# Causal attention on one Trainium2 core: value products of two rounds issued together, projections parted anew between the rounds

## The chip, the cores and the metric

The kernel runs on one NeuronCore of one Trainium2 chip. TensorE multiplies and transposes, VectorE and ScalarE read its results out of PSUM, GpSimd works on SBUF only, and SyncE starts transfers. The metric is the device time of one execution in microseconds (us); less is better. All of the five engines run programs of their own, which meet only through semaphores.

## The reference, cut to what matters

Two decoder layers on x of 2 x 1024 x 256 in float32: a recurrence, a cross attention and a ternary feed forward, then a causal self attention, a second cross attention and a quantized gated feed forward, each followed by a layer norm. The change touches only the causal self attention of the second layer, 16 heads of 64 over 1024 positions, for 2 batches:

```
q = jnp.einsum('qdh,bcd->bhcq', Q, x) * sq
k = jnp.einsum('qdh,bcd->bhcq', K, x) * sq
v = jnp.einsum('vdh,bcd->bhcv', V, x) * sv
att = jnp.einsum('bhcq,bhCq->bhcC', q, k) / d_query
att = jnp.where(causal, att, -jnp.inf)
p = jax.nn.softmax(att, axis=-1)
y = jnp.einsum('bhcC,bhCv->bhcv', p, v)
z = jnp.einsum('dvh,bhcv->bcd', W, y) * (math.sqrt(d_embed / d_value) / num_heads)
x = _layernorm(x + z)
```

## The kernel before

A pair of heads in one batch is a unit u; there are 2 x 8 = 16 units. A unit has eight query tiles qt of 128 rows, and tile qt looks at qt + 1 key blocks of 128. `causal_rounds` (line 1645) packs tiles so that each round has eight key blocks for each of the two heads: (4,2), (5,1), (6,0) and (7) of unit u, then (3) of u together with (3) of u + 1, then (4,2), (5,1), (6,0), (7) of u + 1. These are nine rounds for two units and 72 rounds in all, numbered n = 0 to 71.

One order of steps, written by `causal_order` (line 1535), is walked by every engine; an engine executes the steps for which it has a handler, in that order, and skips the rest. The steps of round n are:

- `cs(n)`: TensorE computes the scores of both heads, 64 x 128 weights, into banks 0 to 3 (line 1742); VectorE adds the causal mask and takes the row maxima, head 0 first (lines 1875 and 1877); ScalarE takes the first exponential (line 1812). A score matmul waits until the exponential of round n - 1 has read the same bank (line 1740).
- `cp(n - 2)`: TensorE multiplies the turned probabilities by the values, two heads side by side in 64 columns each, into bank 6 (line 1767).
- `cn(n, 0)`, `cn(n, 1)`: VectorE takes the reciprocals (line 1888); GpSimd scales head 0 (line 1919), VectorE head 1 (line 1894).
- `ct(n - 1)`: TensorE transposes the 16 blocks of round n - 1 in four groups of four, head 1 first (line 1754). ScalarE copies groups 0 and 1 to SBUF (line 1825), VectorE group 2 (line 1882).
- `ce(n)`: ScalarE takes the other exponentials, head 0 and then head 1, at most two each.
- `cy(n - 2)`: ScalarE copies the result of the value products out of bank 6 (lines 1832 and 1838). `ctl(n - 1)`: ScalarE copies group 3 of the transposes.
- `beside[n]`: the projections of later units: `cq`, `ck`, `cv`, each for half of the 1024 positions (lines 1704, 1715 and 1728; copied out by ScalarE, VectorE and VectorE, lines 1794, 1854 and 1859). There are 12 for nine rounds. Transposes of weights (`flip`) stand there in rounds 10 to 13, and the output products of batch 0 (`zout`, line 1782) with their norm from round 37 on.

Transposes, projections, flips and output products share the three banks 4, 5 and 7 in turn (lines 1579 to 1603): an entry waits for the copy of the third entry before it. So group 3 of `ct` takes the bank of group 0, the first projection behind it that of group 1, and a second one that of group 2.

```
        for key, name, value in ends:
            if key in k.room:
                continue
            n = len(causal) % 3
            causal.append(key)
            k.room[key] = ((4, 5, 7)[n], *free[n])
            free[n] = (name, value)
```

Of the kernel before, what the change touches and what calls it, by code (L numbers as in the profile page):

```python
# [16 lines left out]
P = 128  # L17
# [8 lines left out]
HP = H // 2  # L26
# [36 lines left out]
class Order:  # L63
# [13 lines left out]
    def at(self, *step):  # L77
        return self.number[step]
# [39 lines left out]
def lane_of(L, T):  # L118
    return {0: T % LANES, 1: T // BT, 2: T // BT, 3: 2 + T // BT, 4: T % WIDE, 5: OUTPUTS.index(T) % LANES if T < BT else T % LANES, 6: 0, 7: T % LANES}[L]

# [1414 lines left out]
def causal_order(k):  # L1535
    o = k.order
    n0 = len(k.flips)
    for n, p in enumerate(range(0, HP, 2)):
        k.flip_of("wz", [k.wzp[c][:, q * P:(q + 1) * P] for q in (p, p + 1) for c in range(DC)],
                  k.WzT[:, p:p + 2, :].rearrange("p q d -> p (q d)"), 4 + n % 2, ("vector", "scalar")[n % 2])  # L1540
    wz = [[("wzp",)]] + [[("flip", n)] for n in range(n0, len(k.flips))]
    o.add(("causal_load", 2), ("causal_setup",))

    rounds = causal_rounds()
    beside = [[] for _ in rounds]
    for u in range(0, 2 * HP, 2):
        n = ROUNDS * u // 2
        for gap, x in ((0, ("cq", u + 1, 0)), (0, ("ck", u + 1, 0)), (1, ("cq", u + 1, 1)), (2, ("ck", u + 1, 1)), (3, ("cv", u + 1, 0)), (4, ("cv", u + 1, 1)),
                       (4, ("cq", u + 2, 0)), (5, ("ck", u + 2, 0)), (6, ("cq", u + 2, 1)), (7, ("ck", u + 2, 1)), (8, ("cv", u + 2, 0)), (8, ("cv", u + 2, 1))):
            if x[1] < 2 * HP:  # L1550
                beside[n + gap].append(x)
    for i, steps in enumerate(wz):
        beside[ROUNDS + i] += steps
    ahead = HP // 2 * ROUNDS + 1
    for i, T in enumerate(OUTPUTS):
        chain, n = list(norm_chain(5, T)), ahead + i // 2
        beside[n] += [("zout", T)] + chain[:3]
        beside[n + 1].append(chain[3])
        beside[n + 2] += chain[4:]
    o.add(("cq", 0, 1), ("ck", 0, 1), ("cv", 0, 1))  # L1560
    for n in range(len(rounds)):
        o.add(("cs", n))
        if n >= 2:
            o.add(("cp", n - 2))
        o.add(("cn", n, 0))
        if n >= 1:
            o.add(("ct", n - 1))
        o.add(("ce", n))
        if n >= 2:
            o.add(("cy", n - 2))  # L1570
        if n >= 1:
            o.add(("ctl", n - 1))
        o.add(("cn", n, 1), *beside[n])
    n = len(rounds) - 1
    o.add(("ct", n), ("ctl", n), ("cp", n - 1), ("cy", n - 1), ("cp", n), ("cy", n))
    o.meet()

    k.turned = {by: sum(k.flips[x[1]][4] == by for x in o.steps if x[0] == "flip") for by in ("scalar", "vector")}
    k.piece, causal, free, made = {}, [], [("c.q", 0)] * 3, [0, 0]
    for step in o.steps:  # L1580
        ends = []
        if step[0] in ("cq", "ck", "cv"):
            ends = [(step, "c." + step[0][1], o.at(*step))]
        elif step[0] == "zout" and step[1] < BT:
            ends = [(step, "ln.r", o.at("r", 5, step[1]))]
        elif step[0] == "flip" and k.flips[step[1]][0] == "wz":
            by = k.flips[step[1]][4]
            ends = [(step, "flip." + by, sum(k.flips[x[1]][4] == by for x in o.steps if x[0] == "flip" and x[1] <= step[1]))]
        elif step[0] == "turn" and step[1] == 5 and step[2] < BT:
            ends = [(step, "ln.put", o.at("put", *step[1:]))]  # L1590
        elif step[0] == "ct":
            for i in range(len(causal_groups(step[1]))):
                by = int(i != 2)
                made[by] += 1
                k.piece[step + (i,)] = (("vector", "scalar")[by], made[by], sum(made))
                ends.append((step + (i,), ("c.pT.vector", "c.pT.scalar")[by], made[by]))
# [7 lines that stand above are left out]
# [35 lines left out]


ROUNDS = 9
OUTPUTS = (4, 2, 5, 1, 6, 0, 7, 3)


# [36 lines left out]
def causal_column(n, t):  # L1681

    tiles = causal_rounds()[n]
    return 1 - t if len(tiles) == 2 and tiles[0][0] == tiles[1][0] else t
# [8 lines left out]
def causal_tensor(e, w, k):  # L1693
    sem, at, PS, rounds = k.sem, k.order.at, k.PS, Rounds()
# [62 lines left out]
    def cp(n):  # L1757
        for i in range(len(causal_groups(n))):
            by, m, _ = k.piece["ct", n, i]
            w.wait_ge("c.pT." + by, m)  # L1760
        w.wait_ge("c.y", n)
        for t, u, qt, start in rounds.places(n):
            w.wait_ge("c.v", at("cv", u, qt // 4))
            c = causal_column(n, t) * P
            for j in range(qt + 1):
                for h in range(2):
                    y = e.matmul(PS[h * 64:(h + 1) * 64, 6, c:c + P], k.V[u % 2][:, j, h * 64:(h + 1) * 64], k.pT[n % 2][:, (1 - h) * BT + start + j, :],  # L1767
                                 start=j == 0, stop=j == qt, skip_group_check=True)
        y.then_inc(sem("c.pv"), 1)

    def zout(T):
        t, bank = T % BT, T % 2
        w.wait_ge("c.y", ROUNDS * HP // 2 * (T // BT + 1))
        for by in ("scalar", "vector"):
# [13 lines left out]
def causal_scalar(e, w, k):  # L1788
    sem, at, PS, rounds = k.sem, k.order.at, k.PS, Rounds()
# [3 lines left out]
        w.wait_ge("t2.conv", len(k.conv_pe))  # L1793
        e.mul(k.qT[u % 2][:, blk * 512:(blk + 1) * 512], PS[:, k.room["cq", u, blk][0], :], -1.0 / 256).then_inc(sem("c.q"), 1)

    def cs(n):
        if n >= 2:
            w.wait_ge("c.turn", k.piece["ct", n - 2, len(causal_groups(n - 2)) - 1][2])
        exps(n, 0, (0,))
# [27 lines left out]
    def cy(n):  # L1827
        tiles = rounds.tiles[n]
        (u, qt), (v, low) = tiles[0], tiles[-1]
        w.wait_ge("c.pv", n + 1)  # L1830
        if len(tiles) == 1:
            e.copy(k.YT[:, u % HP, qt * P:(qt + 1) * P], PS[:, 6, 0:P]).then_inc(sem("c.y"), 1)
            return
        if u == v:
            dst = k.YT[:, u % HP, :].rearrange("p (t q) -> p t q", q=P)[:, low:qt + 1:qt - low, :]
        else:
            dst = k.YT[:, u % HP:v % HP + 1, qt * P:(qt + 1) * P]
        e.copy(dst, PS[:, 6, 0:2 * P].rearrange("p (t q) -> p t q", q=P)).then_inc(sem("c.y"), 1)  # L1838

    return {"cq": cq, "cs": cs, "ce": ce, "ct": ct, "ctl": ctl, "cy": cy}  # L1840


def causal_vector(e, w, k):
# [52 lines left out]
    def r(L, T):  # L1896
        w.wait_ge("c.zout", at("zout", T))
        if T in OUTPUTS[LANES:]:
            w.wait_ge("ln.unit", at("unit", 5, OUTPUTS[OUTPUTS.index(T) - LANES]))
# [799 lines left out]
```

## Time and profile before

| | |
|---|---|
| median of 3 runs | 2013.95 us (2013.32 to 2014.62) |
| profiled execution | 2018.72 us |
| its span from the first to the last instruction | 2016.9 us |
| mean granted TensorE clock | 0.924 |
| busy: TensorE matmul | 1747.6 us (87%) |
| busy: VectorE | 1388.2 us (69%) |
| busy: ScalarE | 1014.5 us (50%) |
| busy: GpSimd | 456.4 us (23%) |
| causal rounds 0 to 71 in the profile | about 765 to 1405 us |

Times are in us from the start of the span. In rows of the timeline a group of like instructions is merged; the first number is its start and the second its length. Matmuls are pipelined, so the distance from one group's start to the start of the next is what the group costs, more than its printed length. PE is TensorE's matmul, PEld its weight load, DVE VectorE, ACT ScalarE, POOL GpSimd. READ_ACCUMULATOR rows are the last part of the instruction before them.

### The profile page before, as it was taken

The numbers are of one execution on the slowest core, as the hardware profiler recorded it, in microseconds if no ns is written. First come the engines' busy times: TensorE is split into PE (matmuls) and PEld (weight loads), VectorE is DVE, ScalarE is ACT, GpSimd is POOL, SyncE is SP. The second block draws the span as 40 slices with busy tenths as digits, with TensorE's granted clock in tenths as the row PEclk, the third lists the DMA queues.
The fourth block names the chain that finished last, engine by engine and source line by source line (L and its number), as shares of the span: only waits on it lengthen the run. The fifth ranks groups of instructions, "written<-read, shape, count | busy, mean of one in ns | idle before, by whom it ended". The sixth has DMA issues, their size and how long they took to land.

```text
span 2016.9 us, 34705 instructions
## 1 busy us (share of the span) xinstructions
PE 1747.6 (87%) x12889; PEld 1267.5 (63%) x12889; DVE 1388.2 (69%) x4850; ACT 1014.5 (50%) x2639; POOL 456.4 (23%) x493
## 2 busy tenths in 40 slices
PE   3678988888878889999999999999879999989808
PEld 1356766666653455667667766667559899974307
DVE  6888888887236886777776577776446767653685
ACT  5645556555338534555553455554135545433752
POOL 4000000000000323333343333333113232320003
PEclk8778888888979989999999999999989999999959
DMA  5000000000000101000000000001323342400001
GB/s 160 1 1 1 1 1 1 1 1 1 1 1 22 21 21 69 1 1 1 1 1 1 1 1 1 2 1 38 101 63 78 82 95 65 95 1 0 0 0 42
DMA packets 86078, 49.56 MB, mean 25 GB/s; under 512 B 40223, under 2 KB 83669, under 8 KB 85717
## 3 DMA queue, kind: packets, MB, share of 16 engines
q1 hardware_dynamic: 80195, 47.18, 9.1%
q8 instruction: 102, 1.67, 0.3%
q10 hardware_dynamic: 5714, 0.16, 0.2%
q14 instruction: 67, 0.55, 0.1%
HBM read 45.24 MB, written 2.10 MB: 23 GB/s over the span
## 4 chain that ended last, share of the span: by engine, by line
PE 58%; DVE 27%; ACT 9%; issue 3%; POOL 2%; DMA 1%; ACTq 0%; DVEq 0%; POOLq 0%
PE PS L2063 6%; PE PS L1742 6%; DVE nx L764 6%; DVE sq L773 6%; PE PS L1754 5%; PE PS L1767 4%; PE PS L2481 3%; ACT px L1812 3%; PE PS L1728 3%; PE PS L1704 3%; PE PS L2126 3%; PE PS L1782 2%; PE PS L1715 2%; PE PS L2082 2%; PE PS L2091 2%
## 5 line engine op out<-in xcount | busy, mean ns | idle before, releaser
L1812 ACT ACTIVATE px<-PS,cnm 128x896 f32<-128x896 f32 (+7 forms) x256 | 189.4, 756 | 285.5 <-DVE cnm L1877 285.5
L1919 POOL TENSOR_SCALAR px<-px,crl 128x640 f32<-128x640 f32 (+7 forms) x128 | 232.5, 1826 | 371.2 <-DVE crl L1888 371.2
L773 DVE TENSOR_SCALAR sq<-nx 128x4 f32<-128x4 f32 x1024 | 174.3, 170 | 31.3
L764 DVE TENSOR_TENSOR_SCAN nx<-sq 128x6 f32<-128x6 f32 x1024 | 173.0, 169 | 32.0 <-POOL sq L903 0.9
L1875 DVE TENSOR_REDUCE cm<-PS 128x1 f32<-128x512 f32 (+3 forms) x224 | 153.7, 686 | 44.6 <-PE PS L1742 44.6
L1754 PE MATMUL PS<-ident,px 128*128 128x128 f32 x1152 | 156.1, 281 | 9.3 <-ACT pT L1825 6.2
L198 POOL TENSOR_SCALAR rstd<-mv 128x1 f32<-128x1 f32 x80 | 34.0, 425 | 533.7 <-DVE mv L176 533.7
L2153 ACT ACTIVATE YT<-YT,xnm 128x154 f32<-128x154 f32 x256 | 104.8, 413 | 92.7 <-DVE xnm L2195 92.7
L1742 PE MATMUL PS<-kT,qT 64*128 64x512 f32 (+3 forms) x768 | 147.9, 503 | 0.4
L1754 PEld LDWEIGHTS PS<-ident,px 128*128 128x128 f32 x1152 | 124.1, 141 | 36.6 <-ACT pT L1825 23.9
L1767 PEld LDWEIGHTS PS<-pT,V 128*64 128x64 f32 x2304 | 124.8, 137 | 34.4 <-issue 32.5
L1767 PE MATMUL PS<-pT,V 128*64 128x128 f32 x2304 | 142.1, 276 | 0.6 <-ACT YT L1838 0.6
L1825 ACT COPY pT<-PS 128x512 f32<-128x512 f32 x216 | 122.4, 603 | 7.4 <-PE PS L1754 7.4
L1742 PEld LDWEIGHTS PS<-kT,qT 64*128 64x128 f32 x768 | 67.1, 186 | 80.0 <-issue 44.4
L1894 DVE TENSOR_SCALAR px<-px,crl 128x640 f32<-128x640 f32 (+7 forms) x128 | 108.6, 884 | 2.5
L205 POOL TENSOR_SCALAR rstd<-lst 128x1 f32<-128x1 f32 x48 | 9.3, 194 | 424.4 <-ACT ljunk L264 422.7
L1149 DVE TENSOR_REDUCE nnm<-PS 128x1 f32<-128x154 f32 x256 | 72.7, 308 | 43.2 <-PE PS L1014 42.8
L2242 POOL TENSOR_TENSOR YT<-YT,xrl 128x1024 f32<-128x1024 f32 x32 | 60.8, 1899 | 176.4 <-DVE YT L2204 176.4
L1888 DVE RECIPROCAL crl<-cl 128x2 f32<-128x2 f32 (+1 forms) x144 | 23.8, 165 | 97.5 <-ACT px L1812 97.5
L1877 DVE CUSTOM_DVE_ANT_0 PS<-PS,cmask,cm 128x128 f32<-128x128 f32 x224 | 80.5, 359 | 7.9
L818 PE MATMUL PS<-XT,W1T 128*128 128x256 f32 x256 | 64.9, 399 | 4.2 <-ACT XT L288 2.4
L2208 DVE COPY YT<-PS 128x512 f32<-128x512 f32 x80 | 51.9, 681 | 21.5 <-PE PS L2091 21.5
(339 smaller groups left out, 3882.8 us busy)
## 6 DMA issues: line engine op xcount, KB each, us to landing
xbs<-in_fside_Bx16xSxS SPq DMA_DIRECT2D x8, 1232.0 KB, 6.8
fsrc<-in_fside_Bx16xSxS SPq DMA_DIRECT2D x8, 1232.0 KB, 6.7
xmk<-in_mask_Bx16xSxS_bk SPq DMA_DIRECT2D x8, 308.0 KB, 8.6
fsrc<-in_mask_Bx16xSxS_bk SPq DMA_DIRECT2D x8, 308.0 KB, 8.4
X<-in_x SPq DMA_DIRECT2D x4, 512.0 KB, 6.7
w<-in_L_attn_W_ffn SPq DMA_DIRECT2D x2, 1024.0 KB, 12.6
t<-in_L_ffn_w SPq DMA_DIRECT2D x2, 1024.0 KB, 11.9
out<-xs SPq DMA_DIRECT2D x16, 128.0 KB, 1.7
```

The source lines that it names most:

```text
L764: e.tensor_tensor_scan(k.nx[:, t % 2, :], d0, d1, 0.0, ALU.mult, ALU.add).then_inc(sem("rec.scan"), 1)
L773: e.tensor_scalar(place(c % 2 * 2 * W6 + 6 * n + 7), state, 10.0, -10.0, ALU.min, ALU.max).then_inc(sem("rec.clip"), 1)
L1742: y = e.matmul(PS[:, 2 * h + lo // 512, lo % 512:lo % 512 + hi - lo], k.qT[u % 2][rows_, qt * P:(qt + 1) * P], k.kT[u % 2][rows_, lo - c0: ...
L1754: y = e.transpose(PS[:, bank, q * P:(q + 1) * P], k.px[n % 2][:, h, (starts[t] + j) * P:(starts[t] + j + 1) * P], k.ident[:, :])
L1767: y = e.matmul(PS[h * 64:(h + 1) * 64, 6, c:c + P], k.V[u % 2][:, j, h * 64:(h + 1) * 64], k.pT[n % 2][:, (1 - h) * BT + start + j, :], st ...
L1812: e.activation(k.px[n % 2][:, h, c0:c1], row[:, c0:c1], ACT.Exp, scale=-1.0, bias=k.cnm[:, h, slot:slot + 1], accum_out=k.cl[:, h, slot:sl ...
L1825: e.copy(k.pT[n % 2][:, 4 * i:4 * i + len(group), :].rearrange("p b q -> p (b q)"), PS[:, k.room["ct", n, i][0], 0:len(group) * P]).then_i ...
L1875: e.tensor_reduce(most, row[:, start * P:mid], AX.X, ALU.min).then_inc(sem("c.before"), 1)
L1894: e.tensor_scalar(x, x, k.crl[:, 1, slot + t:slot + t + 1], None, ALU.mult).then_inc(sem("c.normal1"), 1)
L1919: e.tensor_scalar(x, x, k.crl[:, 0, slot:slot + 1], None, ALU.mult).then_inc(sem("c.normal0"), 1)
L2063: y = e.matmul(PS[:, bank, q * P:(q + 1) * P], k.x1w[n][:, c, (4 * hf + q) * P:(4 * hf + q + 1) * P], k.XT[:, c, g * P:(g + 1) * P], start ...
L2153: y = e.activation(k.xS[:, h, :], k.xS[:, h, :], ACT.Exp, scale=-1.0, bias=k.xnm[:, h:h + 1], accum_out=k.xsm[:, h:h + 1])
```

## The change

Value products no longer follow the scores of every round. Even rounds have none; an odd round n issues `cp(n - 3)` and `cp(n - 2)` one after the other, and ScalarE copies the two results one after the other in the same round. Each of the two has its own 256 columns of bank 6, and waits for the copies of the pair before.

ScalarE's first exponential gets a step name of its own (`ca`), so that it can stand elsewhere than the scores. In an even round the order is scores, transposes of round n - 1, all exponentials of round n, reciprocals and scaling. In an odd round it is scores, the two value products, first exponential, transposes of round n - 1, the other exponentials, the two copies of results. For VectorE the copy of group 2 stands, in an even round, directly behind the maxima of round n and ahead of the first reciprocal; in an odd round behind that reciprocal, as before.

The same 12 projections for nine rounds are spread otherwise, by `BESIDE`: every even round (up to 66) has two, an odd round has one or none. Which kinds and halves there are stays the same.

```diff
--- before.py
+++ after.py
@@ -1545,8 +1545,7 @@
     beside = [[] for _ in rounds]
     for u in range(0, 2 * HP, 2):
         n = ROUNDS * u // 2
-        for gap, x in ((0, ("cq", u + 1, 0)), (0, ("ck", u + 1, 0)), (1, ("cq", u + 1, 1)), (2, ("ck", u + 1, 1)), (3, ("cv", u + 1, 0)), (4, ("cv", u + 1, 1)),
-                       (4, ("cq", u + 2, 0)), (5, ("ck", u + 2, 0)), (6, ("cq", u + 2, 1)), (7, ("ck", u + 2, 1)), (8, ("cv", u + 2, 0)), (8, ("cv", u + 2, 1))):
+        for gap, x in zip(BESIDE[n % 2], [(kind, v, blk) for v in (u + 1, u + 2) for kind, blk in (("cq", 0), ("ck", 0), ("cq", 1), ("ck", 1), ("cv", 0), ("cv", 1))]):
             if x[1] < 2 * HP:
                 beside[n + gap].append(x)
     for i, steps in enumerate(wz):
@@ -1559,20 +1558,17 @@
         beside[n + 2] += chain[4:]
     o.add(("cq", 0, 1), ("ck", 0, 1), ("cv", 0, 1))
     for n in range(len(rounds)):
+        turns = [("ct", n - 1)] if n else []
+        ends = [("ctl", n - 1)] if n else []
         o.add(("cs", n))
-        if n >= 2:
-            o.add(("cp", n - 2))
-        o.add(("cn", n, 0))
-        if n >= 1:
-            o.add(("ct", n - 1))
-        o.add(("ce", n))
-        if n >= 2:
-            o.add(("cy", n - 2))
-        if n >= 1:
-            o.add(("ctl", n - 1))
+        if n % 2:
+            pair = range(max(n - 3, 0), n - 1)
+            o.add(*[("cp", m) for m in pair], ("ca", n), ("cn", n, 0), *turns, ("ce", n), *[("cy", m) for m in pair], *ends)
+        else:
+            o.add(*turns, ("ca", n), ("ce", n), ("cn", n, 0), *ends)
         o.add(("cn", n, 1), *beside[n])
     n = len(rounds) - 1
-    o.add(("ct", n), ("ctl", n), ("cp", n - 1), ("cy", n - 1), ("cp", n), ("cy", n))
+    o.add(("ct", n), ("ctl", n), ("cp", n - 1), ("cp", n), ("cy", n - 1), ("cy", n))
     o.meet()
 
     k.turned = {by: sum(k.flips[x[1]][4] == by for x in o.steps if x[0] == "flip") for by in ("scalar", "vector")}
@@ -1639,6 +1635,7 @@
 
 
 ROUNDS = 9
+BESIDE = (0, 0, 2, 2, 3, 4, 4, 6, 6, 7, 8, 8), (0, 1, 1, 3, 3, 4, 5, 5, 6, 7, 7, 8)
 OUTPUTS = (4, 2, 5, 1, 6, 0, 7, 3)
 
 
@@ -1758,10 +1755,10 @@
         for i in range(len(causal_groups(n))):
             by, m, _ = k.piece["ct", n, i]
             w.wait_ge("c.pT." + by, m)
-        w.wait_ge("c.y", n)
+        w.wait_ge("c.y", n - n % 2)
         for t, u, qt, start in rounds.places(n):
             w.wait_ge("c.v", at("cv", u, qt // 4))
-            c = causal_column(n, t) * P
+            c = n % 2 * 2 * P + causal_column(n, t) * P
             for j in range(qt + 1):
                 for h in range(2):
                     y = e.matmul(PS[h * 64:(h + 1) * 64, 6, c:c + P], k.V[u % 2][:, j, h * 64:(h + 1) * 64], k.pT[n % 2][:, (1 - h) * BT + start + j, :],
@@ -1793,7 +1790,7 @@
         w.wait_ge("t2.conv", len(k.conv_pe))
         e.mul(k.qT[u % 2][:, blk * 512:(blk + 1) * 512], PS[:, k.room["cq", u, blk][0], :], -1.0 / 256).then_inc(sem("c.q"), 1)
 
-    def cs(n):
+    def ca(n):
         if n >= 2:
             w.wait_ge("c.turn", k.piece["ct", n - 2, len(causal_groups(n - 2)) - 1][2])
         exps(n, 0, (0,))
@@ -1827,17 +1824,18 @@
     def cy(n):
         tiles = rounds.tiles[n]
         (u, qt), (v, low) = tiles[0], tiles[-1]
-        w.wait_ge("c.pv", n + 1)
+        y = PS[:, 6, n % 2 * 2 * P:(n % 2 + 1) * 2 * P]
+        w.wait_ge("c.pv", n - n % 2 + 2)
         if len(tiles) == 1:
-            e.copy(k.YT[:, u % HP, qt * P:(qt + 1) * P], PS[:, 6, 0:P]).then_inc(sem("c.y"), 1)
+            e.copy(k.YT[:, u % HP, qt * P:(qt + 1) * P], y[:, 0:P]).then_inc(sem("c.y"), 1)
             return
         if u == v:
             dst = k.YT[:, u % HP, :].rearrange("p (t q) -> p t q", q=P)[:, low:qt + 1:qt - low, :]
         else:
             dst = k.YT[:, u % HP:v % HP + 1, qt * P:(qt + 1) * P]
-        e.copy(dst, PS[:, 6, 0:2 * P].rearrange("p (t q) -> p t q", q=P)).then_inc(sem("c.y"), 1)
-
-    return {"cq": cq, "cs": cs, "ce": ce, "ct": ct, "ctl": ctl, "cy": cy}
+        e.copy(dst, y.rearrange("p (t q) -> p t q", q=P)).then_inc(sem("c.y"), 1)
+
+    return {"cq": cq, "ca": ca, "ce": ce, "ct": ct, "ctl": ctl, "cy": cy}
 
 
 def causal_vector(e, w, k):
```

## Rows read from the trace of the kernel before

**Rows 1.** Chain that ended last, from the page: share of the span by engine.

```profile
PE 58%; DVE 27%; ACT 9%; issue 3%; POOL 2%; DMA 1%; ACTq 0%; DVEq 0%; POOLq 0%
```

**Rows 2.** Busy time by stretch: us, PE, PEld, DVE, ACT, POOL busy, clock, DMA.

```profile
765.00:1405.00 640.00, 627.32 (x5109) 440.08 (x5107) 449.44 (x1177) 336.10 (x840) 238.93 (x144) 1.00 0.01 3
958.65:1034.15 75.50, 74.96 (x625) 51.90 (x624) 54.84 (x144) 41.64 (x104) 29.02 (x17) 1.00 0.01 1
```

**Rows 3.** Timeline of TensorE matmuls: start, length, line, out<-in, count; rounds 25 and 27.

```profile
974.60 2.00 PE L1742 MATMUL PS<-kT,qT 64*128 64x512 f32 x12
976.52 1.97 PE L1767 MATMUL PS<-pT,V 128*64 128x128 f32 x32
978.42 2.18 PE L1754 MATMUL PS<-ident,px 128*128 128x128 f32 x16
980.44 1.98 PE L1715 MATMUL PS<-XT,wkT 128*128 128x512 f32 x4
982.35 1.99 PE L1742 MATMUL PS<-kT,qT 64*128 64x512 f32 x8
...
997.78 1.98 PE L1704 MATMUL PS<-XT,wqT 128*128 128x512 f32 x4
...
1001.41 1.78 PE L1742 MATMUL PS<-kT,qT 64*128 64x512 f32 x10
```

**Rows 4.** Timeline of round 4, where ScalarE is free when transposes end.

```profile
799.84 1.99 PE L1754 MATMUL PS<-ident,px 128*128 128x128 f32 x16
800.53 1.07 ACT L1825 COPY pT<-PS 128x512 f32<-128x512 f32 x2 [0.57 <-PE PS L1754]
...
801.49 0.70 ACT L1812 ACTIVATE px<-PS,cnm 128x512 f32<-128x512 f32 x1
801.66 2.05 PE L1728 MATMUL PS<-wvT,XT 128*128 128x128 f32 x16
```

**Rows 5.** Waits, 765 to 1405: who for whom, us in total, times, longest.

```profile
PEld PS L1754 <- ACT pT L1825: 23.9, 63, 2.8
...
PEld PS L1715 <- DVE pT L1882: 1.9, 7, 0.3
```

**Rows 6.** Timeline of VectorE: maxima of rounds 25, 26, 27; copy of group 2.

```profile
976.62 0.96 DVE L1875 TENSOR_REDUCE cm<-PS 128x1 f32<-128x768 f32 x1 [0.51 <-PE PS L1742]
...
979.65 0.14 DVE L1877 DVE_READ_ACCUMULATOR2_ANT cnm<- 128x1 f32 x1
...
980.92 0.67 DVE L1882 COPY pT<-PS 128x512 f32<-128x512 f32 x1
...
984.37 1.09 DVE L1875 TENSOR_REDUCE cm<-PS 128x1 f32<-128x896 f32 x1 [0.51 <-PE PS L1742]
...
987.17 0.14 DVE L1877 DVE_READ_ACCUMULATOR2_ANT cnm<- 128x1 f32 x1
...
993.97 0.69 DVE L1875 TENSOR_REDUCE cm<-PS 128x1 f32<-128x512 f32 x1 [1.23 <-PE PS L1742]
...
997.43 0.14 DVE L1877 DVE_READ_ACCUMULATOR2_ANT cnm<- 128x1 f32 x1
```

**Rows 7.** Timeline of rounds 68 and 69, which have no projections.

```profile
1372.58 0.60 ACT L1812 ACTIVATE px<-PS,cnm 128x384 f32<-128x384 f32 x1
1372.85 3.24 PE L1742 MATMUL PS<-kT,qT 64*128 64x512 f32 x12
...
1373.15 0.81 ACT L1812 ACTIVATE px<-PS,cnm 128x640 f32<-128x640 f32 x1
...
1373.83 0.23 ACT L1812 ACTIVATION_READ_ACCUMULATOR px<-PS,cnm 128x1 f32 x1
...
1374.10 0.30 PEld L1742 LDWEIGHTS PS<-kT,qT 64*128 64x128 f32 x4 [0.96 <-ACT px L1812]
...
1374.85 1.67 DVE L1894 TENSOR_SCALAR px<-px,crl 128x640 f32<-128x640 f32 x2
1376.02 1.73 PEld L1767 LDWEIGHTS PS<-pT,V 128*64 128x64 f32 x32 [0.33 <-issue]
```

## The prediction

> **What bounds the kernel now.** I read the chain that ended last first: TensorE holds 58% of it and VectorE 27% [rows 1]. Then the busy times by stretch: in the 640 us of the causal rounds TensorE is busy for 627, VectorE for 449, ScalarE for 336, at full clock; nine rounds with their twelve projections take 75.50 us, of which TensorE is busy 74.96 [rows 2]. So TensorE sets the pace here, and a saving must shorten its sequence without letting another engine take its place. The timeline of the matmuls gives the price of each part as the distance to the next start [rows 3]: scores 1.92, value products 1.90, transposes 2.02, one projection behind them 1.91, two projections 3.63 (997.78 to 1001.41). The second projection adds only 1.72, so a change of kind of work costs about 0.19 and the work itself about 1.72.
>
> Transposes cost 1.82 where ScalarE is idle as they end: 799.84 to 801.66 [rows 4]. Elsewhere group 3 waits for ScalarE's copy of group 0, which stands behind an exponential; 63 such waits sum to 23.9 us [rows 5]. The reader is to see that this, some 0.2 to 0.6 us a round, is TensorE's largest loss in this stage.
>
> Behind TensorE stands a second chain that is nearly as long: scores, VectorE's maxima, exponentials, and then the scores of the next round, which need the PSUM banks. Rounds 68 and 69 have no projections and show it bare: the scores started at 1372.85 stop until head 1's first exponential has ended, the next weights load at 1374.10, and the next kind of work starts at 1376.02, 1.92 later [rows 7].
>
> **The change, part by part: what it saves.** Value products in pairs cost 1.90 + 1.72 = 3.62 rather than 3.80. The trace has no such pair; the nearest row is that of two projections, and the bounds are 3.80 (no saving) and 3.44 (twice the saving). I take 3.62, since the lone value product carries the same surplus as the lone projection. Transposes cost 1.82 everywhere: in an even round ScalarE copies groups 0 and 1 while it would otherwise wait for the maxima, in an odd round the first exponential is long done. Without any new wait an even round would take 1.92 + 1.82 + 3.63 = 7.37, an odd one with a projection 1.92 + 3.62 + 1.82 + 1.91 = 9.27, and one without 1.92 + 3.62 + 1.82 + about 0.05 = 7.41. Eighteen rounds (two units' nine twice) have nine even rounds, six odd ones with a projection and three without: 144.2 against 2 x 75.50 = 151.0. Over 72 rounds that is 27 us.
>
> The Trainium skill ("TensorEngine Tiling (Array Packing)", Key Properties) says that changing the tiling mode, not just the tile, drains TensorE. By that rule the pairs save one change in two rounds. It agrees with the 0.19 above. By that rule alone, with this 0.19, 35 pairs would gain 6.7 us.
>
> **New wait 1: the second projection of an even round.** It takes the bank of transpose group 2, which VectorE copies. With the value products gone from the even round, the transposes start 1.92 after the scores start and the second projection is due at 1.92 + 1.82 + 1.81 = 5.55. But VectorE's copy of group 2 stands behind all maxima of the new round. Those start 2.02 after the scores (976.62 - 974.60) and last 3.17, 2.94 and 3.60 in rounds 25, 26 and 27 [rows 3, 6]; the two kinds not shown have four reductions as round 27 has, so over nine rounds the mean is (5 x 3.60 + 2 x 3.17 + 2 x 2.94) / 9 = 3.36. The copy starts 0.06 before the printed end of the last read and takes 0.67 [rows 6]; add 0.04 to the release of the load (the step seen from the exponential's end, 1374.06, to 1374.10 [rows 7]) and 1.91 for the projection: the even round lasts s + 3.36 + 2.56, where s is the start of the maxima. s is 2.02 where VectorE is free. Behind an odd round its scaling of head 1 (1.67, starting 0.24 after the last exponential [rows 7]) and a key or value copy can run longer, and s is then up to 2.45; a round (3,3) may begin its maxima earlier. Worked through the nine even rounds, the mean is 2.06. So an even round takes 7.98, not 7.37. Today the same wait is nearly nothing: 1.9 us in seven waits [rows 5]. Behind the waiting projection stand the next scores and all of TensorE.
>
> **New wait 2: the odd round without a projection.** Transposes start at 1.92 + 3.62 = 5.54, and ScalarE's step behind its first exponential waits for them: the remaining exponentials start 1.65 after the transposes do (799.84 to 801.49 [rows 4]), where they could have run 1.6 earlier. Head 0's second one takes 0.57 (1372.58 to 1373.15) and head 1's first 0.91 (1373.15 to 1374.06) [rows 7]; for the other kinds the two sum to nearly the same. The next scores are thus free at 5.54 + 1.65 + 1.48 + 0.04 = 8.71; call it 8.70. TensorE would be there at 7.41. With one projection it is there at 9.27, and nothing is lost.
>
> **Small parts.** The two result copies stand together behind the exponentials and ahead of group 3's copy; the consumers of group 3 come a round later, so I cost them nothing, and if that cover went they would cost the 0.3 to 0.4 of a copy. In round 37 the first output product waits for the results of round 35, which are now copied at about 9.9 of that round, not before 8.8: 1.1 us, once. GpSimd's scaling is finished before its transposes by over 0.1 in every kind of round; it is not on the path. The last four rounds have no projections; odd ones get dearer (8.7 against about 7.4), even ones cheaper (6.6 to 7.0), and at the end only one result copy lies between the last products and the meeting: together I take +1, with -1 and +3 as bounds. Semaphores, DMAs and the work outside the stage do not change, and no DMA is moved.
>
> **Sum.** Eighteen rounds: 9 x 7.98 + 6 x 9.27 + 3 x 8.70 = 71.8 + 55.6 + 26.1 = 153.5, against 151.0. Four times 2.5 is 10, and 1.1 + 1 gives 12 us. The profiled execution of 2018.7 would be 2030.7; the median of the runs is 4.8 lower, so I forecast 2026.
>
> **Rivals.** (a) The waits stay hidden and the change gives what it saves: 2014 - 27 + 2 = 1989. Against it: both waits follow from the order of VectorE's and ScalarE's steps, with durations from rows. It decides if VectorE's copy of group 2 is over by 5.5 of an even round, which needs maxima that end 1.5 earlier than any row shows. Faster also if only the wait for the second projection stays hidden and the odd one comes: 12 x (8.70 - 7.41) = 15.5, so 2004. (b) Only the wait of the even rounds comes, since ScalarE's late exponentials in the odd rounds are caught up: 36 x 0.61 = 22, so 2014 - 25 + 22 = 2011, no change. For it speaks that only 14 of 36 odd rounds are bare; against it rows 7, where just this stall shows. (c) VectorE becomes the bound: it is busy 449 of 640 us, and now the scaling of an odd round, a projection's copy and the maxima crowd where the two rounds meet. If every pair loses 0.5 more, s being 2.5 throughout, that is 36 x 0.5 = 18: 2044. (d) The pair does not do what it is said to: no saving between two value products adds 35 x 0.18 = 6: 2032, inside the forecast's own spread.
>
> The Trainium skill ("TensorEngine Tiling (Array Packing)", PSUM Bottleneck) says that PSUM copies may become the bottleneck once TensorE is sped up. This case's trace shows that only at the ring's waits so far. The rule points to the forecast and to (c), and what it would give is theirs.
>
> **How the numbers follow.** Forecast with (d): 0.62, its own range 2018 to 2036, from the bounds of the pair (6 us each way), of the last rounds and of s. (a) 0.14 with its half case, (b) 0.14, (c) 0.10. A measurement of this kernel can tell about 0.2% (4 us) from no change. Faster 0.14, same 0.14, slower 0.72. The range takes in (b) and the half case and most of (c): 2004 to 2040.
>
> **What would show it.** In the profile after: value products in groups of 64 matmuls with 3.6 to the next start; transposes at 1.82; the weight load of the second projection in even rounds (keys, queries or values) idle for about 0.5 on VectorE's copy, some 34 times; scores at 8.7 after those before in odd rounds without projections, their loads idle on the exponential; waits of transposes for ScalarE's copies nearly gone. It is wrong if the second projection in even rounds starts at 5.5, if bare odd rounds last 7.5, or if even rounds last over 8.5.

## The result and the profile after

The changed kernel takes 2031.76 us (median of 4, 2030.97 to 2037.62), the kernel before 2013.64 us beside it; the ratio is 1.0095 with a 95% interval of 1.0076 to 1.0115. It is slower by about 19 us (18 between the medians). I had forecast 2026, slower by 12. Its profiled execution took 2030.97 us, with a span of 2029.1.

The chain by engine has hardly moved (PE 58% and DVE 27% in [rows 1]):

```profile
PE 58%; DVE 28%; ACT 8%; issue 3%; POOL 2%; DMA 0%; ACTq 0%; POOLq 0%; DVEq 0%
```

Busy time by stretch says more. The columns are those of [rows 2]. The first line is the whole stage, from the first scores of round 0 to the first output product behind the last value product; the others are rounds 18 to 26 and 27 to 35. First the changed kernel, then the kernel before over the same rounds:

```profile
757.38:1417.01 659.63, 633.37 (x5106) 450.15 (x5105) 434.65 (x1178) 344.59 (x840) 237.57 (x145) 0.98 0.01 3
913.83:989.21 75.38, 73.79 (x594) 51.11 (x593) 52.38 (x144) 42.63 (x104) 27.78 (x16) 1.00 0.01 1
989.21:1066.93 77.72, 76.38 (x658) 54.16 (x657) 52.74 (x144) 42.88 (x105) 29.72 (x17) 1.00 0.00 1
```

```profile
765.41:1405.26 639.85, 626.91 (x5105) 439.82 (x5105) 449.51 (x1178) 336.22 (x840) 238.98 (x145) 1.00 0.01 3
916.44:991.94 75.50, 74.96 (x626) 51.90 (x625) 54.85 (x143) 41.64 (x104) 29.02 (x16) 1.00 0.01 1
991.94:1067.42 75.48, 74.95 (x625) 51.90 (x624) 54.83 (x143) 41.64 (x104) 29.02 (x16) 1.00 0.01 1
```

The stage is 19.8 us longer, about what the ratio says of the whole kernel. The two profiled executions differ by only 12.2 (spans of 2029.1 and 2016.9), since the stage began 8.0 earlier in that of the changed kernel, whose instructions up to there are the same. That this profiled execution took 2031.0, where the sum of the prediction has 2030.7, is therefore luck. Eighteen steady rounds take 153.1 in the place of 151.0, with TensorE idle for 2.9 instead of 1.1. And the mean granted clock of the stage is 0.98 instead of 1.00, which the steady rounds do not show: something happens elsewhere.

The two forecast waits are there. Round 28 of the changed kernel is an even round with two projections (L1712 keys, L1701 queries; L1751 transposes; L1880 is VectorE's copy of group 2; columns as in [rows 3]):

```profile
1000.43 1.99 PE L1751 MATMUL PS<-ident,px 128*128 128x128 f32 x16
1002.26 1.98 PE L1712 MATMUL PS<-XT,wkT 128*128 128x512 f32 x4
1003.99 0.14 DVE L1875 DVE_READ_ACCUMULATOR2_ANT cnm<- 128x1 f32 x1
1003.99 0.69 DVE L1880 COPY pT<-PS 128x512 f32<-128x512 f32 x1
1004.73 0.30 PEld L1701 LDWEIGHTS PS<-XT,wqT 128*128 128x128 f32 x2 [1.32 <-DVE pT L1880]
1004.74 1.98 PE L1701 MATMUL PS<-XT,wqT 128*128 128x512 f32 x4 [0.50 <-DVE pT L1880]
1006.65 0.70 PE L1739 MATMUL PS<-kT,qT 64*128 64x512 f32 x2
```

The reader is to see that the first projection costs 2.48 to the next start, not 1.82: the copy starts with the last read of the maxima, and the load of the second projection follows its end. The round takes 8.14. Round 29 is an odd round without a projection:

```profile
1008.58 3.71 PE L1764 MATMUL PS<-pT,V 128*64 128x128 f32 x64
1012.22 1.99 PE L1751 MATMUL PS<-ident,px 128*128 128x128 f32 x16
1012.91 1.07 ACT L1822 COPY pT<-PS 128x512 f32<-128x512 f32 x2 [1.45 <-PE PS L1751]
1014.14 3.23 PE L1739 MATMUL PS<-kT,qT 64*128 64x512 f32 x8
1014.23 1.02 ACT L1809 ACTIVATE px<-PS,cnm 128x896 f32<-128x896 f32 x1
1015.12 0.22 ACT L1809 ACTIVATION_READ_ACCUMULATOR px<-PS,cnm 128x1 f32 x1
1015.39 0.30 PEld L1739 LDWEIGHTS PS<-kT,qT 64*128 64x128 f32 x4 [0.96 <-ACT px L1809]
```

Two value products cost 3.64. ScalarE idles 1.45 for the transposes, takes its copies, and only then the exponentials; the next scores go on at 1015.39, which is 8.74 after this round's scores began at 1006.65. The loss of the second projections is in the waits between 765 and 1430 too (columns as in [rows 5]):

```profile
PEld PS L1701 <- DVE pT L1880: 14.1, 8, 3.2
...
PEld PS L1712 <- DVE pT L1880: 10.9, 9, 1.5
...
PE PS L1701 <- DVE pT L1880: 7.5, 8, 2.3
PEld PS L1751 <- ACT pT L1822: 7.3, 5, 2.8
...
PE PS L1712 <- DVE pT L1880: 3.3, 6, 0.7
```

The waits of the transposes for ScalarE fell from 23.9 us in 63 to 7.3 in 5, as the change promised, and those of the query and key projections for VectorE rose from 1.9 [rows 5] to 25.0. These are idle times of the weight load, part of which lies under matmuls that still run: the matmuls themselves idled 10.8 (7.5 and 3.3).

In rounds 5 to 35 and 45 to 66, by the distance to the next start, transposes went from 109.7 to 97.4 us and value products from 100.6 to 98.4, a gain of 14.5 (with 54 value products counted against 53, since the pairs stand in odd rounds); scores went from 101.9 to 112.6 and projections from 131.6 to 144.0, a loss of 23.1.

### The profile page after: what moved, and what is told of

It reads as the page before. It is cut to its first block, busy times and chain, and to the rows that moved or that the text cites. A ratio compares the mean times of both kernels' runs of the same rounds, so it can differ in the third digit from the quotient of the medians.

```text
span 2029.1 us, 34675 instructions
## 1 busy us (share of the span) xinstructions
PE 1744.8 (86%) x12889; PEld 1269.5 (63%) x12889; DVE 1371.4 (68%) x4850; ACT 1023.2 (50%) x2639; POOL 454.8 (22%) x493
## 4 chain that ended last, share of the span: by engine, by line
PE 58%; DVE 28%; ACT 8%; issue 3%; POOL 2%; DMA 0%; ACTq 0%; POOLq 0%; DVEq 0%
PE PS L1764 7%; PE PS L1739 6%; PE PS L2061 6%; DVE nx L764 6%; DVE sq L773 6%; PE PS L1751 4%; PE PS L2479 3%; PE PS L1779 3%; PE PS L1725 3%; PE PS L2124 3%; PE PS L2080 2%; PE PS L1701 2%; PE PS L1712 2%; DVE cm L1873 2%; ACT px L1809 2%
## 5 line engine op out<-in xcount | busy, mean ns | idle before, releaser
L1739 PE MATMUL PS<-kT,qT 64*128 64x512 f32 (+3 forms) x768 | 162.4, 513 | 4.3 <-ACT px L1809 3.0
L1751 PE MATMUL PS<-ident,px 128*128 128x128 f32 x1152 | 145.5, 280 | 4.6 <-ACT pT L1822 4.6
L1751 PEld LDWEIGHTS PS<-ident,px 128*128 128x128 f32 x1152 | 125.2, 142 | 30.8 <-issue 19.8
L1764 PE MATMUL PS<-pT,V 128*64 128x128 f32 x2304 | 135.9, 277 | 0.0
L1739 PEld LDWEIGHTS PS<-kT,qT 64*128 64x128 f32 x768 | 72.6, 189 | 83.7 <-issue 48.2
L1892 DVE TENSOR_SCALAR px<-px,crl 128x640 f32<-128x640 f32 (+7 forms) x128 | 96.9, 793 | 2.5
L1701 PE MATMUL PS<-XT,wqT 128*128 128x512 f32 x128 | 64.6, 628 | 8.0 <-DVE pT L1880 7.5
```

The source lines that it names most:

```text
L1701: y = e.matmul(PS[:, bank, :], k.wqkv[0][:, c, pair * P:(pair + 1) * P], k.XT[:, c, b * S + blk * 512:b * S + (blk + 1) * 512], start=c == ...
L1739: y = e.matmul(PS[:, 2 * h + lo // 512, lo % 512:lo % 512 + hi - lo], k.qT[u % 2][rows_, qt * P:(qt + 1) * P], k.kT[u % 2][rows_, lo - c0: ...
L1751: y = e.transpose(PS[:, bank, q * P:(q + 1) * P], k.px[n % 2][:, h, (starts[t] + j) * P:(starts[t] + j + 1) * P], k.ident[:, :])
```

## The clock, which the prediction left out

In three places the changed kernel has a lowered granted clock (the column before the last two). The rows show the scores of round 2, the first output products in round 37, and the scores and value products of round 71; behind the stretches shown the rest of round 2 is at 0.79, and round 71 falls again to 0.65.

```profile
770.64:775.60 4.96, 4.88 (x13) 2.66 (x13) 2.64 (x6) 2.13 (x7) 3.50 (x2) 0.60 0.00 0
1084.69:1093.48 8.79, 8.79 (x32) 7.17 (x32) 2.23 (x5) 0.44 (x1) 2.78 (x4) 0.81 0.00 0
1396.20:1399.90 3.70, 3.70 (x6) 1.17 (x6) 3.27 (x6) 0.77 (x3) 2.63 (x2) 0.50 0.02 4
1399.90:1405.10 5.20, 5.20 (x66) 5.02 (x65) 1.53 (x4) 1.21 (x2) 2.84 (x1) 0.70 0.00 0
```

0.50 is the lower of the clock's two levels, 1.2 GHz; the figure of a longer stretch is its mean. Each of the three places follows a gap of TensorE. In round 37 it is the wait for ScalarE's copies of the results, which I had priced as a wait alone:

```profile
1084.69 8.86 PE L1779 MATMUL PS<-WzT,YT 128*128 128x256 f32 x32 [2.07 <-ACT YT L1830]
```

The eight products behind it took 8.79 in the place of 7.10 before. The runs below put this to the test.

## The experiments

The theory after the result: wait 1 (second projection for VectorE's copy behind the maxima), wait 2 (next scores for exponentials behind the transposes' copies), and, at the ends and in round 37, gaps behind which the clock is lower. The rivals: VectorE as a whole is the bound; or one half of the change, the pairing or the parting, carries the loss by itself. The time of the stage, from the traces, with the same start and end as above (18 rounds: rounds 18 to 35; end: from the scores of round 68):

| kernel | ratio to before, interval | stage | rounds 0 to 8 | 18 rounds | 36 to 44 | end |
|---|---|---|---|---|---|---|
| before | 1 | 639.85 | 73.23 | 150.98 | 107.87 | 38.49 |
| changed | 1.0095 (1.0076 to 1.0115) | 659.63 | 75.73 | 153.10 | 111.37 | 42.63 |
| a_g3vec | 1.0039 (1.0024 to 1.0053) | 646.03 | 74.68 | 148.90 | 110.53 | 42.86 |
| b_expfirst | 0.9994 (0.9985 to 1.0003) | 637.95 | 73.67 | 149.70 | 106.95 | 36.02 |
| c_both | 0.9974 (0.9962 to 0.9985) | 633.31 | 72.52 | 145.64 | 107.86 | 42.57 |
| d_oldpart | 1.0016 (1.0006 to 1.0027) | 646.00 | 71.42 | 151.59 | 108.44 | 40.90 |
| e_newpart_only | 1.0074 (1.0058 to 1.0091) | 656.26 | 78.49 | 153.95 | 110.69 | 38.50 |
| f_ends | 0.9946 (0.9932 to 0.9961) | 629.68 | 71.94 | 145.64 | 107.83 | 39.56 |
| g_cy37 | 1.0104 (1.0089 to 1.0119) | 655.76 | 75.72 | 153.11 | 107.51 | 42.61 |
| h_oldpart_both | 0.9980 (0.9970 to 0.9989) | 639.25 | 73.24 | 151.34 | 104.73 | 36.21 |
| j_paired_end | 0.9942 (0.9921 to 0.9963) | 629.52 | 70.29 | 145.64 | 106.31 | 42.58 |
| k_single_end | 0.9940 (0.9915 to 0.9964) | 629.85 | 71.96 | 145.63 | 107.95 | 39.59 |

The stage is the finer measure: what lies outside it moved by up to 8 us between executions (it began anywhere from 757.38 to 765.41), while in two executions of the changed kernel the stage took 659.63 and 659.54. It isn't free of chance either: rounds that are the same in two kernels differed by 3.3 us in one case, which is told with l_both_again, so a difference of 3 us between two stages says little without the rounds that it comes from.

**a_g3vec: wait 1 away.** In even rounds ScalarE copies group 2 and VectorE group 3, whose bank nobody needs before the next round.

```diff
-                by = int(i != 2)
+                by = int(i != 2 + step[1] % 2)
...
-        for i in range(2):
+        for i in range(2 + n % 2):
             turned(n, i)
...
-        turned(n, 3)
+        if n % 2 == 0:
+            turned(n, 3)
```

> The changed kernel (2031.8 us), with one edit: in even rounds ScalarE copies transpose group 2 and VectorE group 3, so that the bank which the second projection takes is free before the maxima. Theory (the second projection waits for VectorE's copy behind the maxima): even rounds fall to 7.4 us each, the projections of rounds 5 to 35 and 45 to 66 from 144 to about 132 us in sum, the whole to about 2015. Rival (VectorE as a whole is the bound, and the wait only moves): the time stays above 2027 and scores or transposes wait in the place of the projection.

The ratio fell to 1.0039 and the stage by 13.6 us; projections of the counted rounds took 130.8 us instead of 144.0, scores and transposes 112.6 and 97.4 as before. Nothing moved into their place, so VectorE as a whole is not the bound: the rival has fallen. Round 28 of this kernel:

```profile
1001.26 1.98 PE L1712 MATMUL PS<-XT,wkT 128*128 128x512 f32 x4
...
1003.00 0.69 DVE L1882 COPY pT<-PS 128x512 f32<-128x512 f32 x1
1003.07 1.88 PE L1701 MATMUL PS<-XT,wqT 128*128 128x512 f32 x4
```

The second projection starts 1.81 after the first, while VectorE's copy has only begun. The forecast of 2015 was 17 us of gain; eighteen rounds gained 4.2, four times that is 16.8. Rounds 0 to 8 and 36 to 44 gave back only 1.05 and 0.84, and the end nothing. In rounds 36 to 44 the clock took part of the gain: round 43 took 10.62 at 0.87 where it had taken 9.31 at 1.00.

**b_expfirst: wait 2 away.** In an odd round without projections, the second exponential of head 0 and the first of head 1 come before the copies of the transposes (`cb` and `cc` are `ce` split in two).

```diff
+            bare = not any(x[0] in ("cq", "ck", "cv") for x in beside[n])
+            middle = [("cb", n), *turns, ("cc", n)] if bare else [*turns, ("cb", n), ("cc", n)]
-            o.add(*[("cp", m) for m in pair], ("ca", n), ("cn", n, 0), *turns, ("ce", n), *[("cy", m) for m in pair], *ends)
+            o.add(*[("cp", m) for m in pair], ("ca", n), ("cn", n, 0), *middle, *[("cy", m) for m in pair], *ends)
...
```

> The changed kernel, with one edit: in odd rounds that have no projection ScalarE takes the second exponential of head 0 and the first of head 1 ahead of the copies of the transposes. Theory (the next scores wait for exponentials that stand behind those copies): these rounds fall from 8.7 to about 7.8, scores of rounds 5 to 35 and 45 to 66 from 112.6 to about 104, the whole to about 2019. Rival (the maxima or the transposes are late there, and the order of ScalarE does not matter): 2029 or more, since group 3 of the transposes then waits for ScalarE's copy of group 0.

The ratio is 0.9994, so this edit alone undoes the loss. The scores of the counted rounds are back at 101.9 us (I had expected 104), transposes rose by 1.1 to 98.5, and the stage is shorter by 21.7, more than the 13 I had expected of it. Round 23:

```profile
958.48 0.79 ACT L1814 ACTIVATE px<-PS,cnm 128x640 f32<-128x640 f32 x1 [0.28 <-DVE cnm L1880]
...
959.26 1.06 ACT L1827 COPY pT<-PS 128x512 f32<-128x512 f32 x2
959.89 0.42 PEld L1753 LDWEIGHTS PS<-ident,px 128*128 128x128 f32 x4 [0.22 <-ACT pT L1827]
...
960.48 1.78 PE L1741 MATMUL PS<-kT,qT 64*128 64x512 f32 x10
```

The exponential of head 1 is over before the copies start; the rival's wait of group 3 is there, at 0.2 us. Of the 21.7 us, 3.4 came from rounds 18 to 35 and as much from rounds 45 to 62, 6.6 from the end, 4.4 from rounds 36 to 44, 2.1 from rounds 0 to 8 and the rest from the other rounds. In round 37 the wait ahead of the output products is 0.73 in the place of 2.07, and they took 7.10 at clock 1.00; round 71 is at 1.00 too.

**c_both: both.**

> Both edits together. Theory: the gains add, since they lie in different rounds: about 2002, faster than the kernel before by 12. Rival (the second chain of scores, maxima and exponentials takes over once TensorE's two waits are gone): 2010 or more.

The ratio is 0.9974, faster than the kernel before by about 5 us and not by 12. In the steady rounds the gains add: 18 rounds get shorter by 4.2 with the one edit, by 3.4 with the other and by 7.5 with both, so the rival of a second chain taking over falls. What is missing is mainly the end, 42.57 where b_expfirst has 36.02, and round 43, which took 10.94 at clock 0.84 and in b_expfirst 9.30 at 1.00.

**g_cy37: does the gap lower the clock?** In round 37 alone the two `cy` stand before the transposes' copies.

```diff
+            early = [("cy", m) for m in pair]
+            late = [] if n == ahead else early
+            early = early if n == ahead else []
-            o.add(..., ("cn", n, 0), *turns, ("ce", n), *[("cy", m) for m in pair], *ends)
+            o.add(..., ("cn", n, 0), *early, *turns, ("ce", n), *late, *ends)
```

> The changed kernel, with one edit: in round 37 alone ScalarE copies the results of rounds 34 and 35 before the transposes, so that the first output product need not wait for them. In the changed kernel that product waits 2.07 us and then the granted clock is 0.81 over the eight products, which take 8.79 us where they took 7.10 at clock 1.00. If the wait is what costs the clock, both go: round 37 falls from 18.4 to 14.6, the whole by about 3.5 to 2028. If the clock falls for another reason, only the wait goes: 2029.7 and the products still take 8.8.

Round 37 fell from 18.41 to 14.56, by 3.85: the wait of 2.07 and the products' surplus of 1.7 went together. Its eight products:

```profile
1085.90:1092.97 7.07, 7.07 (x34) 5.96 (x33) 3.40 (x8) 2.13 (x7) 4.22 (x4) 1.00 0.00 1
```

With the gap gone the clock stays at 1.00, as foreseen if the wait is what costs the clock. But the wait doesn't bring the fall by itself. In a_g3vec the same products stand behind the same wait, and take 7.11 from start to start of what follows, at clock 1.00:

```profile
1080.90 7.17 PE L1779 MATMUL PS<-WzT,YT 128*128 128x256 f32 x32 [2.07 <-ACT YT L1831]
```

What a_g3vec lacks is the wait of 0.50 in the round before, ahead of the second projection of round 36. The clock fell only where both waits stood, in both executions of the changed kernel; one execution each with only the first (this kernel) or only the second (a_g3vec) doesn't make this a rule.

The whole time does not show it: the ratio of 1.0104 (1.0089 to 1.0119) is not below the changed kernel's 1.0095, although the stage is 3.9 us shorter in the trace. The rest of the kernel varies by more than that.

**d_oldpart and e_newpart_only: one half of the change each.** In d the projections are parted as before, with the pairing; in e the value products follow each round's scores as before, with the new parting.

```diff
-BESIDE = (0, 0, 2, 2, 3, 4, 4, 6, 6, 7, 8, 8), (0, 1, 1, 3, 3, 4, 5, 5, 6, 7, 7, 8)
+BESIDE = ((0, 0, 1, 2, 3, 4, 4, 5, 6, 7, 8, 8),) * 2
```

> The change's pairing and its order of steps, with the projections parted between rounds as before (2,1,1,1,2,1,1,1,2 per nine rounds, odd and even alike); the kinds follow in the change's order, and the first unit's too. Theory (two waits, in whatever round they fall): no odd round is bare except the last two, but an even round with one projection is too short for the second chain and lasts 6.7, not 5.65, and two-projection even rounds still wait for VectorE's copy. Eighteen rounds take about 153, as in the changed kernel, and the whole some 2028 to 2035. Rival (the new parting is what costs the time): 2016 or less.

> The kernel before, with the new parting of projections alone: a value product follows the scores of every round. Theory: even rounds with two projections take 9.5 as such rounds did, the twelve bare odd ones are held by the second chain at about 7.4 where TensorE has only 5.8 of work; eighteen rounds take 154, the whole about 2028. Rival (the pairing is what costs the time): 2016 or less.

For e the theory held: 1.0074, eighteen rounds 153.95 where 154 was expected. For d it did not: the ratio is 1.0016, near the rival's "2016 or less" (2017.59 was measured), and the stage is 13.6 us shorter than the changed kernel's. Eighteen rounds take 151.59, not 153; the start, rounds 36 to 44 and the end are shorter by 4.3, 2.9 and 1.7. Taken this way, 13.6 of the 19.8 us go with the new parting and 6.2 stay with the pairing. Taken the other way, the new parting alone costs 16.4 (e), and 3.4 are left for the pairing: the two halves overlap and can't be parted cleanly. A part of d's short start may be chance: its round 1 took 9.52 at clock 1.00, and with the same steps 10.36 at 0.92 in h_oldpart_both. The waits that d was expected to have are there, only smaller. In the even rounds with one projection the second chain stands at the next scores (round 29 of d):

```profile
1004.07 0.30 PEld L1739 LDWEIGHTS PS<-kT,qT 64*128 64x128 f32 x2 [0.76 <-ACT px L1809]
1005.12 0.30 PEld L1739 LDWEIGHTS PS<-kT,qT 64*128 64x128 f32 x4 [0.75 <-ACT px L1809]
```

**h_oldpart_both: is the parting needed?** Both edits on the old parting.

> Both edits of the earlier run on the old parting of projections. Theory: the parting is needed, since an even round has no value products and one projection does not fill it; eighteen rounds take about 152 against 145.6 with the new parting, the whole about 1.3% above the run with both edits, so about 1% above the kernel before. Rival (parting is indifferent once the waits are gone): within 0.3% of the run with both edits.

Eighteen rounds take 151.34 against 145.64 with the new parting. The parting that loses in the changed kernel is worth 5.7 us in eighteen rounds once the two waits are away, since an even round without value products needs two projections to fill it. The whole did not show the expected 1.3%: the ratio is 0.9980, where the rival's 0.3% of c holds, and the stage is 5.9 us longer than c's. Rounds 45 to 62 lose 5.7 as well and rounds 0 to 17 lose 2.2, but rounds 36 to 44 are 3.1 shorter than in c (1.6 of it is the clock in round 43), and the end takes 36.21 where that of c takes 42.57, with the same steps. That is the next point.

**l_both_again and i_changed_again: is the clock a matter of the execution?** The kernel with both edits and the changed kernel, unaltered.

> The kernel with both edits once more. In its profile round 69 took 12.51 us at clock 0.70 and 0.66, while the kernel with the old parting and the same steps for these rounds took 9.46 at full clock. If that belongs to the program, rounds 68 to the end take 42.6 again; if to the single execution, they may take about 36.

> The changed kernel once more, unaltered, for its clock in rounds 2, 37 and 71. If the dips belong to the program (a gap at a fixed place), round 2 lasts 11.6 and round 37 18.4 again, each within 0.2. If they belong to the single execution, at least one of them is gone.

Neither changed. The changed kernel's rounds 2 and 37 lasted 11.63 and 18.41 again, its stage 659.54; the stage of the kernel with both edits took 633.31 twice. The scores and the value products of round 69, in c_both, in l_both_again, and in h_oldpart_both:

```profile
1354.75:1359.87 5.12, 4.51 (x12) 2.09 (x13) 3.54 (x10) 1.95 (x6) 3.44 (x2) 0.70 0.00 0
1359.87:1365.35 5.48, 5.48 (x66) 5.31 (x65) 2.84 (x13) 2.44 (x6) 2.40 (x2) 0.65 0.00 0
```

```profile
1358.77:1363.88 5.11, 4.50 (x13) 2.09 (x13) 3.55 (x10) 1.95 (x6) 3.44 (x2) 0.71 0.00 0
1363.88:1369.37 5.49, 5.49 (x66) 5.32 (x65) 2.83 (x13) 2.44 (x6) 2.42 (x2) 0.65 0.00 0
```

```profile
1367.49:1371.13 3.64, 3.04 (x12) 1.46 (x12) 2.67 (x9) 1.96 (x6) 2.17 (x2) 1.00 0.00 0
1371.13:1374.78 3.65, 3.65 (x66) 3.48 (x65) 3.51 (x14) 1.45 (x4) 1.27 (x1) 1.00 0.00 0
```

The steps of rounds 68 and 69 are the same in all three, but the first two lose 3.3 us to the clock and the third none. What TensorE did in the rounds before differs, and so does the execution.

So these two kernels repeated their dips. That a dip belongs to the program alone doesn't follow, and two of the kernels below speak against it: j_paired_end and k_single_end are the same up to round 67 and ran on the same chip. Behind the wait of round 1, which is 2.55 in both, the projection and the scores of round 2 start 1.90 apart in j and 2.75 in k (first j, then k):

```profile
773.05 0.66 PE L1756 MATMUL PS<-ident,px 128*128 128x128 f32 x4 [2.55 <-ACT pT L1831]
773.55 1.98 PE L1706 MATMUL PS<-XT,wqT 128*128 128x512 f32 x4
775.45 2.00 PE L1744 MATMUL PS<-kT,qT 64*128 64x512 f32 x12
```

```profile
776.71 0.66 PE L1758 MATMUL PS<-ident,px 128*128 128x128 f32 x4 [2.55 <-ACT pT L1833]
777.20 2.81 PE L1708 MATMUL PS<-XT,wqT 128*128 128x512 f32 x4
779.95 2.81 PE L1746 MATMUL PS<-kT,qT 64*128 64x512 f32 x12
```

In k this projection and these scores ran at a granted clock of 0.69, in j at 1.00. Round 43 took 10.93 at 0.84 in k and 9.30 at 1.00 in j. Together these rounds are 3.3 us longer in k, with the same instructions. So some dips repeat from execution to execution and others don't, and which gap brings one is not settled by these runs. Whether h_oldpart_both keeps its end at 1.00 each time is not known from its single trace.

**f_ends, j_paired_end, k_single_end: a faster kernel.** f_ends is c with one projection of the first unit moved to round 1 and a value product in each of the last four rounds. j is c with that projection and with the results copied early in round 37. k is f with the early copies.

```diff
+        if n >= 68:
+            o.add(("cp", n - 2), ("ca", n), ("cn", n, 0), *turns, ("cb", n), ("cc", n), ("cy", n - 2), *ends)
+        elif n % 2:
...
-        w.wait_ge("c.pv", n - n % 2 + 2)
+        w.wait_ge("c.pv", n - n % 2 + 2 if n < 66 else n + 1)
```

> Both edits of the earlier run, and the two ends of the stage put as in the kernel before: the last four rounds have a value product each, and one projection of the first unit goes to round 1. Theory (in the ends TensorE runs dry, and its clock falls behind each gap): rounds 68 to the end fall from 42.6 to about 38.5 us, rounds 1 and 2 from 18.3 to about 17.3, the whole is about 0.25% below the run with both edits, so 0.5% below the kernel before. Rival (the ends' loss is in the exponentials and not in the clock): rounds 68 to the end stay above 41.5.

> Both edits, one projection of the first unit in round 1, the results copied early in round 37, and the change's paired order kept to the end. Theory: the stage takes 629 if the clock dips in the last rounds as in the first run with both edits, 623 if not; the whole 0.5 to 0.8% below the kernel before. Rival (the single products of the last rounds were what helped): no faster than the run with both edits, 0.26% below the kernel before.

> As the other, but with a value product in each of the last four rounds: 628 us for the stage, the whole 0.6% below the kernel before. Rival (round 37 was hidden): as the run without the early copies, 0.54% below.

f_ends takes 0.9946 of the time before, 0.5% less, as expected. Its end is 39.56, a little over the forecast 38.5, and rounds 1 and 2 take 16.8. j and k are at 0.9942 and 0.9940, not told apart from f or from each other. Their stages are alike for two reasons that cancel: the single value products of the last rounds shorten the end from 42.58 (j) to 39.59 (k), and k lost 3.3 us to the clock in rounds 1, 2 and 43, which are the same in both. In round 37 the early copies did nothing, as k's rival had it: there the exponentials stand ahead of the transposes' copies, and moving the results' copies in front pushed those back. TensorE now waits in group 3 (round 37 of j):

```profile
1069.23 1.09 ACT L1831 COPY pT<-PS 128x512 f32<-128x512 f32 x2
1069.89 0.42 PEld L1756 LDWEIGHTS PS<-ident,px 128*128 128x128 f32 x4 [1.25 <-ACT pT L1831]
```

## Why the prediction was right, and where it was short

- **Direction and mechanism: right.** Both new waits are where the prediction put them, and each was taken away by an edit of its own that moved its own term and little else (a: projections 144.0 to 130.8; b: scores 112.6 to 101.9, with transposes 1.1 up).
- **The saving: right.** Two value products cost 3.64 (3.62 forecast), transposes 1.82 in both kinds of round.
- **Steady rounds: right within 0.4 us in 153.** An odd round with a projection takes 9.33 (9.27 forecast), one without 8.74 (8.70), an even round 7.88 (7.98), if the 1.25 that the next scores wait behind a bare round is given to that round. Eighteen rounds cost 2.1 more than before, not 2.5. Four times that is 8.5 of the 19.8 us. The wait of the even rounds is a mean, though: of rounds 18 to 34 six have it, with 0.2 to 1.0 us (the first projection costs 2.48 in round 18, 2.79 in round 24), and rounds 22, 26 and 30 have next to none, where the sum has 0.61 in each; the waits show 17 loads of queries and keys held by VectorE's copy, not some 34. The prediction let VectorE's copy start 0.06 before the printed end of the last read, which its rows do not show; it starts 0.14 before (1003.99 in round 28).
- **The step that was short: the small parts.** I gave round 37, the start and the end together 2.1 us. What lies beyond the steady rounds' rate took about 11. In round 37 I foresaw the products at 9.9 of the round against 8.8 before, 1.1 us. They started at 9.62, but those of the kernel before had started at 7.90 (1084.79), so the wait cost 1.7, and at clock 0.81 they took 1.7 more: the round is 3.4 longer. The scores of round 2 ran at 0.60 behind the gaps in round 1; I had costed the start of the stage at nothing, and rounds 0 to 8 are 2.5 longer. In round 71 clocks of 0.50 and 0.70 came on top of the dearer last rounds: the end is 4.1 longer, not 1. How the 11 divide between the clock and the waits themselves is measured in round 37 only. The prediction had no term for the clock, though the kernel before also dips in its last rounds.
- **Rival (a)**, a gain, is out by the two waits. **(b)**, only the wait of even rounds, is out: the bare rounds lost what rows 7 had shown, and b_expfirst alone won it all back. **(c)**, VectorE as the bound, is out by a_g3vec. The sentence of the Trainium skill that the prediction puts beside it ("TensorEngine Tiling (Array Packing)", PSUM Bottleneck) is about copies behind a TensorE made four times faster by tiling; no run here shows such a case. **(d)**, no saving by the pair, is out by 3.64.
- The sentence from the Trainium skill ("TensorEngine Tiling (Array Packing)", Key Properties), that a change of tiling mode drains TensorE, agrees with the 3.64 of a pair against twice 1.90: 0.16 less for one change of kind.
- A case I had not asked about: how the loss divides between the two halves of the change. The even rounds' wait needs both that the value products left the even round and that a second projection stands in it: e_newpart_only, which has only the second, has projections of 129.8 us in the counted rounds. The bare round exists only because its projection left, and e has that loss in full (scores 112.6, as in the changed kernel). With the old parting the pairing cost 6.2 us, not 19.8.

## What to carry to other kernels

When work of one engine is moved out of a stretch, list what the other engines do in that stretch in program order, and see which copy now frees a bank later than it is wanted. Here the whole loss hung on two orders on ScalarE and VectorE; with both mended, and the ends filled, the same idea makes the kernel 0.5% faster than the one before. A new gap of the matmul engine can have a second price, the work behind it at the lower clock; since the same gap did not always bring it, it belongs in the range of a forecast, not in its sum.

## What the runs showed of the hardware

- Behind a gap of TensorE the granted clock can be lower: in both executions of the changed kernel the eight output products of round 37 took 8.79 us at 0.81 behind a wait of 2.07 (2.06 in the second), 1.7 us more than at 1.00. With the wait gone the clock row reads 1.00.
- A gap of its own does not decide it. In a_g3vec the same 2.07 us ahead of the same products left the clock at 1.00 and the products at 7.11. The kernel before waited 2.54 us at 778.07 in round 1 and kept 1.00 (its row stands below). Rounds 68 and 69 with loads idle 1.35 and 1.43 kept 1.00 in h_oldpart_both; with 1.34 and 1.44 in c_both the work behind them ran at 0.70.
- Nor do the instructions alone. The changed kernel and c_both repeated their dips in a second execution (659.63 and 659.54, 633.31 and 633.31 us for the stage), but rounds 1, 2 and 43, the same in j_paired_end and k_single_end, took 24.5 us in the one and 27.8 in the other.

The transposes of round 1 in the kernel before:

```profile
778.07 0.66 PE L1754 MATMUL PS<-ident,px 128*128 128x128 f32 x4 [2.54 <-ACT pT L1825]
```
